# A fused attention and mixture-of-experts block on one core: in TensorE's program each chunk issues the front's products first, then the expert tile's

## The reference, cut to what matters

```python
x = layernorm(x + attention(x))                 # 16 x 256 tokens, D = 128
h = x + layernorm(x, ln1) @ attn_w.T
t = layernorm(h, ln2)                           # 4096 tokens
top_vals, top_idx = top_k(t @ gate_w.T, 2)
rw = softmax(top_vals)
out = sum over experts e of comb[:, e] * ((silu(t @ gate_e.T) * (t @ up_e.T)) @ down_e.T)   # inner width 512
x = layernorm(x + (h + out))
```

## The kernel before

| chunk | front products of TensorE | what they need of others |
|---|---|---|
| 48, 56, 64 | context(2g), qk(2g+1), turn_n1(g-1) | probability copy and values copy (ScalarE `late`, chunk before), x1 |
| 49, 57, 65 | scores(2g+1), attn_w even | query and key copy (ScalarE `late`, chunk before); `y_done` of residual(2g) (VectorE `early`, same chunk) |
| 50, 58, 66 | attn_w odd | nothing new |
| 51, 59, 67 | turn_prob(2g+1), values(2g+1) | softmax (ScalarE `late`, chunk before) |
| 52, 60, 68 | context(2g+1), qk(2g+2) | as 48 |
| 53, 61 | scores(2g+2) | as 49, first part |
| 46, 54, 62, 70, 78 | rank(g-1) | choose (VectorE `late`, chunk before) |
| 47, 55, 63 | turn_prob(2g+2), values(2g+2) | as 51 |

## Time and profile before

### The profile page before, as it was taken

One profiled execution on the slowest core, in us unless ns is written; L12 is line 12 of the kernel. 1 busy time (PEld: TensorE's weight loads), 2 busy tenths in 40 slices (PEclk: granted clock), 3 DMA queues, 4 the chain that ended last, 5 costly groups with the idle time before them and its releaser, 6 DMA issues.

```text
span 361.8 us, 8735 instructions
## 1 busy us (share of the span) xinstructions
PE 314.5 (87%) x2052; PEld 271.0 (75%) x2052; DVE 256.4 (71%) x1039; ACT 239.0 (66%) x559; POOL 201.8 (56%) x243
## 2 busy tenths in 40 slices
PE   4878697668899989998999899899999999984970
PEld 3767487446789878887888788688888888873860
DVE  3468969789698869886987988767666766630660
ACT  2679656536867677686768677677777777750471
POOL 0245378857467655773786687686444433342760
PEclk9989989959999999999999999999999999996996
DMA  7178821133212121112112212332211111005931
GB/s 260 54 238 255 287 76 39 46 80 123 55 45 83 40 62 52 46 39 55 52 56 54 67 47 69 89 96 65 63 50 46 36 45 39 15 14 188 334 119 58
DMA packets 27872, 31.97 MB, mean 88 GB/s; under 512 B 4769, under 2 KB 21413, under 8 KB 27824
## 3 DMA queue, kind: packets, MB, share of 16 engines
q1 hardware_dynamic: 23504, 22.88, 21.1%
q0 software_dynamic: 4320, 8.53, 7.2%
HBM read 20.16 MB, written 11.68 MB: 88 GB/s over the span
## 4 chain that ended last, share of the span: by engine, by line
PE 68%; DVE 11%; issue 6%; ACT 5%; POOL 4%; DMA 3%; POOLq 0%; ACTq 0%; SPq 0%; DVEq 0%
PE bank L548 17%; PE bank L496 9%; PE bank L498 8%; PE bank L497 8%; PE bank L534 8%; PE bank L433 3%; PE bank L449 2%; PE bank L703 2%; PE bank L558 2%; POOL expert_rows L1360 2%; PE bank L697 2%; PE bank L473 2%; PE bank L410 1%; DVE hid L1203 1%; ACT xs L748 1%
## 5 line engine op out<-in xcount | busy, mean ns | idle before, releaser
L1369 POOL DMA_INDIRECT moe_rows<-ysb,xrow x71 | 70.4, 992 | 87.2 <-ACT ysb L774 80.7
L548 PE MATMUL bank<-wd,hidT 128*128 x568 | 76.4, 277 | 4.6 <-ACT t L781 3.9
L1360 POOL DMA_INDIRECT expert_rows<-rows,place x64 | 63.0, 985 | 23.7 <-issue 13.4
L548 PEld LDWEIGHTS bank<-wd,hidT 128*128 128x128 f32 x568 | 68.9, 192 | 7.3 <-issue 7.2
L496 PE MATMUL bank<-w_hi,t_hi 128*128 x142 | 63.3, 446 | 6.1 <-DVE hid L1203 4.0
L498 PE MATMUL bank<-w_hi,t_lo 128*128 x142 | 56.7, 399 | 0.0
L497 PE MATMUL bank<-w_lo,t_hi 128*128 x142 | 56.3, 397 | 0.0
L787 ACT ACTIVATE th<-bank 128x512 f32<-128x512 f32 x71 | 42.6, 600 | 15.4 <-PE bank L498 15.2
L1203 DVE SCALAR_TENSOR_TENSOR hid<-th,bank 128x512 f32<-128x512 f32 x71 | 48.3, 681 | 3.2 <-ACT th L787 3.2
L1207 DVE TENSOR_TENSOR hid<-hid,bank 128x512 f32<-128x512 f32 x71 | 48.8, 687 | 2.4
L800 ACT ACTIVATE hidT<-bank 128x512 f32<-128x512 f32 x71 | 42.6, 599 | 10.5 <-PE bank L534 10.2
(11 more groups left out here) (159 smaller groups left out, 570.4 us busy)
## 6 DMA issues: line engine op xcount, KB each, us to landing
xrow<-expert_rows SPq DMA_DIRECT2D x71, 66.0 KB, 1.9
w_raw<-weights SPq DMA_DIRECT2D x16, 256.0 KB, 4.1
w_lo<-moe_rows SPq DMA_DIRECT2D x16, 256.0 KB, 5.4
xT<-xt SPq DMA_DIRECT2D x8, 256.0 KB, 4.9
wd<-weights SPq DMA_DIRECT2D x4, 512.0 KB, 8.9
out<-xs SPq DMA_DIRECT2D x16, 128.0 KB, 1.7
xs<-x SPq DMA_DIRECT2D x3, 512.0 KB, 4.9
moe_rows<-ysb,xrow POOLq DMA_INDIRECT x71, 2.3
```

Of the source, the lines that this page charges most:

```text
L548: last = mm(ps_y, hidT[i % 2][:, c * P:(c + 1) * P], wd[:, bass.ds(w + c * P, P)], start=(c == 0), stop=(c == NC - 1))
L1360: G.indirect_dma_start(out=expert_rows[:, :], out_offset=bass.IndirectOffsetOnAxis(ap=place[:, i, k:k + 1], axis=0), in_=rows[:, i, k, :], ...
L1369: G.indirect_dma_start(out=moe_rows[:, :], out_offset=bass.IndirectOffsetOnAxis(ap=xrow[i % XR][:, C_DST:C_DST + 1].bitcast(I32), axis=0), ...
```

## The change

In TensorE's loop over the chunks the two calls change places.

```diff
             for q in range(STEADY, ALL):
+                front(q)
                 experts(q)
-                front(q)
```

## The result

The changed kernel takes 391.34 us (median of 4 runs, 390.05 to 392.22) against 365.16 us for the kernel before on the same chip (4 runs): a ratio of 1.0713, with a 95% interval of 1.067 to 1.0756. It is slower by 26.2 us, and the forecast was 25 us.

A forecast was written before the change was run, and what follows sets the result against it. TensorE was taken as the bound. Stalls of 32.2 us plus 2.7 for restarts, less 9.8 removed, give +25.1: profiled 363.7 becomes 388.8, and a median 1.3 above gives 390 us; 8-in-10 range 381 to 399.

The forecast's parts named there:

- The stalls: New waits of TensorE's front products for inputs from ScalarE and VectorE: 32.2 us at 27 places.
- half clock: TensorE at 1.2 GHz after long stalls; at most 1.7 us per fall, none taken in the sum.
- restarts: Slower first product group after each TensorE stall: 27 x 0.1, 2.7 us added.
- turn_prob, 6: turn_prob waits for softmax in chunks 47, 51, 55, 59, 63, 67: 0.8 us each, 4.9 in all.
- context, 6: context waits for probability and values copy in chunks 48, 52, 56, 60, 64, 68: 0.9 us each, 5.4 in all.
- scores and attn_w, 8: scores (49, 53, 57, 61, 65) wait for query and key copies, 4.0 us; attn_w (49, 57, 65) for the residual, 6.9.
- rank, 5: rank waits for choose: 1.45 us in chunks 46, 54, 62, 78 and 2.9 in 70, 8.7 in all.
- chunks 72 to 74: turn_n1 of 72 waits 1.4 us, attn_w of 73 waits 0.5, and 0.4 stays in 74: 2.3 together.
- removed: Old TensorE waits for t and hid, with restarts and small unprinted delays, that go away: 9.8 us.
- Waking: A TensorE product starts about 0.25 to 0.27 us behind the end of what releases it.
- the rival named: Clock falls after the long stalls of chunks 49, 57, 65 and 70, 1.7 us each: 397 us; chance 0.25.
- the rival that gave 355: Inputs of front(q) are ready before TensorE needs them, so only the 9.8 us gain is left; chance 0.03.

The follow-up runs named there:

- run with filled waits: Changed kernel with five products of constants, results unused, in front of the even attn_w of chunks 49, 57 and 65: 387.30 us.
- the run with three edits: Changed kernel with rank and the even attn_w back behind experts(q) and ScalarE's copy hidT behind late(q): 365.98 us, ratio 1.0031 to the kernel before.
- the last version: Changed kernel; rank, even attn_w behind experts(q), hidT behind late(q), plan_tiles three chunks later for groups 3 to 5: 375.28 us, ratio 0.9917 to before.
- rank back: Changed kernel with only rank (chunks 46, 54, 62, 70, 78) moved back behind experts(q): 382.91 us.

## Why the prediction was right, point by point

The forecast of 390 was 1.3 us off and its range held the time. The stalls, nearly all of the sum, came where and as forecast; that the total fits so closely is partly luck. The half clock was put at nothing and cost 7.4 us in the profile; against it the restarts were 2.7 too much, 1.2 more of the old losses went than forecast, and the median of the changed kernel lies 0.9 us below its profiled execution, where the forecast put it 1.3 above. By the profiled executions it was 388.8 against 392.22. All sizes here are by the lengths of chunks, less 2.85 and less the issue time of the front.

| term | predicted, us | measured in the profile, us |
|---|---|---|
| turn_prob, 6 | 4.9 | 4.3 |
| context, 6 | 5.4 | 5.0 |
| scores and attn_w, 8 | 4.0 + 6.9 | 1.7 (53, 61) + 10.6 (49, 57, 65) |
| rank, 5 | 8.7 | 8.3 |
| chunks 72 to 74 | 2.3 | 2.4 |
| restarts | 2.7 | in the rows above |
| half clock | 0 | 7.4 |
| removed | -9.8 | -11 |
| net | +25.1 | +28.5 |

- **The stalls.** Places, releasers and order were as forecast. Waking was over-rated: softmax ends at 94.58 and turn_prob starts at 94.64, 0.06 and not 0.27 later; context starts 0.14 behind the values copy. In its place the first group of products behind a wait is slower: scores in chunk 49 last 1.13 against 1.03, context 1.13 against 1.06 in the earlier trace rows. The two nearly offset (over 28 places by the items, not 27), so that the separate restarts should not have been added: the rows above add up to 32.3, the forecast without restarts to 32.2. Within that, turn_prob, context and rank came 0.4 to 0.6 lower each, and scores with attn_w 1.4 higher (12.3 for 10.9), of which 0.5 is attn_w of chunk 49 running at half clock. That ScalarE's copy is the cause is shown by the run with the copy behind late(q), that plan_tiles is the cause of attn_w's wait by the run with plan_tiles behind the residual.
- **rank.** 1.46, 1.40, 1.42 and 1.43 us where 1.45 was said, and 2.6 in chunk 70 where 2.9 was.
- **The clock.** The reading of the kernel before was a little short: there, too, half the clock was granted until 82.5 us, through the first chunks of the loop. The sum took no fall, and this term failed: the profiled execution has all four that the rival named, 2.45, 1.7 and 1.7 us behind attn_w and 1.6 behind rank in 70 and the chunk after. The price of at most 1.7 us for a fall was too low for the first, behind which the clock stayed low for two stretches. The rival's time was not right either: it said 397 for these four falls, since it added them to a sum with the restarts in it and to a median above the profile. The run with filled waits gives the three falls behind attn_w 5.7 us of the profile and 4 of the median, and with the count of filled and unfilled waits above it shows that the idle time brings them. The section of the Trainium skill that was cited (page "TensorE: Matmul & The Clock Gate", "A second HAM failure mode: psum-queue depth-cycling") would have the clock swing with the frequent short idles too; by this trace it did not, for chunks 51 to 56 with 0.4 to 1.1 us of waiting each kept the full clock.
- **What goes away.** 11 us for 9.8, found as what is left between the other rows and the net. This was right in the changed kernel, but the reading "it is won if the stalls go" (the rival that gave 355) was too simple: the run with three edits has no stall of the front and does not win it. Once TensorE is earlier, VectorE is late behind plan_tiles. Only with plan_tiles in a lighter chunk did a part of it, 3 of the 9.8 us, appear.
- **Nothing gives it back** held: the expert chunks behind 82 are as long as before, and the loss stays to the end.

## What to carry to other kernels

When two engines run the same hand-made loop, look at where each input of a step is produced relative to the *other* engine's waiting instruction: a step that moves ahead of the work behind which its inputs are made changes a hidden dependency into a stall each round, here 0.5 to 3.8 us in 25 chunks. Before moving steps on the bound engine, move what would be in front of their inputs on the producers' queues; one order is only good with the other, as the copy showed (1.3% worse in the old order, 6.6 us better in the new one). A long wait of TensorE can cost more than its length, since the clock may fall behind it. And when two orders are compared over a stretch, the stretch has to hold the same work in both: 0.9 us too many in one of them hid a quarter of the gain of the last version.

## What the runs showed of the hardware that was not expected

- Useless products in three long waits of TensorE made the kernel 4 us faster; TensorE kept 2.4 GHz (the granted clock is 1.00 of full from 105.5 to 243 us of that trace).
- Behind the wait of chunk 49 (2.40 us) the clock stayed at 1.2 GHz through two stretches (107.58 to 114.41), though TensorE was busy 2.56 of 3.41 us in the first. Behind waits of 2.39 us it stayed low for one stretch (chunk 57 of the changed kernel) or did not fall (the same chunk with rank back).
- How long TensorE's product starts behind the end of the instruction that it waited for goes by the product in this trace, not by the other engine: 0.05 to 0.06 us for turn_prob and scores (behind ScalarE) and for rank (behind VectorE's `member`, 90.70 to 90.76), 0.14 to 0.15 for context (behind ScalarE) and attn_w (behind VectorE, 108.28 to 108.43), 0.24 for gate (behind `hid`). Why is open.
- The kernel before took 365.4 us on one chip and 382.7 on the same one half an hour later, and 378.0 on another; what stops several engines at once there was not tried.
